# A two-layer transformer block on one core: where the low parts of the weights, one product, the first head copies and one mix stand in the engines' orders

## Time and profile before

| | |
|---|---|
| median of 3 runs | 876.03 us |
| profiled execution | 876.34 us |
| its span | 874.6 us |
| PE busy | 806.8 us (92%) |
| DVE busy | 667.3 us (76%) |
| ACT busy | 579.4 us (66%) |
| POOL busy | 422.2 us (48%) |
| mean granted PE clock | 0.985 |

### The profile page before, as it was taken

How to read it: one execution, slowest core, us unless ns; L and a number is a source line. 1 busy time by engine, 2 the same in 40 slices (tenths; PEclk the granted TensorE clock), 3 DMA queues, 4 the chain that set the end, 5 groups by cost and what they waited for, 6 DMA issues and landing times.

```text
span 874.6 us, 20901 instructions
## 1 busy us (share of the span) xinstructions
PE 806.8 (92%) x7097; PEld 677.9 (78%) x7097; DVE 667.3 (76%) x2136; ACT 579.4 (66%) x1232; POOL 422.2 (48%) x725
## 2 busy tenths in 40 slices
PE   4876999999999999899999999999998999999994
PEld 3554778888888899667777777777766988999984
DVE  5987889888896555778898888979886463487657
ACT  2777868687787533677878777777766233366646
POOL 0353223233253311576767667676765357355423
PEclk9899999999999999999999999999999899999998
DMA  7111220201001010111010211201013112345444
GB/s 218 35 40 43 80 86 12 87 14 37 26 1 49 25 38 25 43 34 31 22 55 23 63 42 37 66 22 43 23 59 120 37 64 95 92 129 134 128 161 170
DMA packets 55017, 54.86 MB, mean 63 GB/s; under 512 B 18209, under 2 KB 49185, under 8 KB 54914
## 3 DMA queue, kind: packets, MB, share of 16 engines
q1 hardware_dynamic: 51506, 44.18, 17.1%
q0 software_dynamic: 3408, 9.34, 3.1%
HBM read 32.85 MB, written 20.65 MB: 61 GB/s over the span
## 4 chain that ended last, share of the span: by engine, by line
PE 68%; DVE 15%; ACT 9%; issue 6%; POOL 1%; DMA 1%; DVEq 0%; ACTq 0%; SPq 0%; POOLq 0%
PE ps L448 13%; PE ps L449 12%; PE ps L450 12%; PE ps L992 10%; PE ps L1003 5%; PE ps L684 3%; PE ps L731 2%; DVE G L2182 2%; PE ps L771 2%; PE ps L976 2%; DVE wu_rows L2182 2%; ACT G L1596 1%; PE ps L1249 1%; PE ps L753 1%; PE ps L1213 1%
## 5 line engine op out<-in xcount | busy, mean ns | idle before, releaser
L2568 POOL TENSOR_SCALAR_AFFINE_SELECT G<-G 128x256 f32<-128x256 f32 x128 | 75.9, 617 | 150.1 <-ACT G L1422 149.9
L1596 ACT ACTIVATE G<-ps 128x512 f32<-128x512 f32 x184 | 102.7, 602 | 39.9 <-PE ps L992 38.3
L448 PE MATMUL ps<-WU 128*128 128x256 f32 x384 | 116.3, 303 | 11.4 <-DVE WU L1977 6.5
L2616 POOL TENSOR_SCALAR G<-G,small 128x256 f32<-128x256 f32 x214 | 99.8, 483 | 51.6 <-DVE small L2182 49.9
L2182 DVE CUSTOM_DVE_ANT_0 G<-ps,nb 128x256 f32<-128x256 f32 x296 | 108.3, 420 | 10.6 <-PE ps L731 9.4
L449 PE MATMUL ps<-WU 128*128 128x256 f32 x384 | 108.3, 282 | 0.0
L450 PE MATMUL ps<-WU 128*128 128x256 f32 x384 | 108.3, 282 | 0.0
L2616 POOL TENSOR_SCALAR wu_rows<-wu_rows,small 128x256 f32<-128x256 f32 x154 | 71.7, 482 | 38.7 <-DVE small L2182 37.7
L448 PEld LDWEIGHTS ps<-WU 128*128 128x128 f32 x384 | 72.8, 190 | 18.0 <-DVE WU L1977 7.3
L992 PE MATMUL ps<-ident,G 128*128 128x128 f32 x592 | 83.5, 278 | 3.0 <-ACT G L1596 2.9
L2182 DVE CUSTOM_DVE_ANT_0 wu_rows<-ps,nb 128x256 f32<-128x256 f32 x216 | 79.5, 420 | 7.4 <-PE ps L731 6.5
(11 more groups left out here) (267 smaller groups left out, 2356.2 us busy)
## 6 DMA issues: line engine op xcount, KB each, us to landing
xs<-G SPq DMA_DIRECT2D x8, 645.0 KB, 6.6
G<-xs SPq DMA_DIRECT2D x39, 128.0 KB
G<-x SPq DMA_DIRECT2D x17, 256.0 KB, 3.1
G<-in_x SPq DMA_DIRECT2D x16, 256.0 KB, 2.8
wu_rows<-yy SPq DMA_DIRECT2D x8, 512.0 KB, 7.0
x<-G SPq DMA_DIRECT2D x15, 256.0 KB, 2.2
wu_rows<-in_wu SPq DMA_DIRECT2D x8, 384.0 KB, 4.9
wraw<-in_wu SPq DMA_DIRECT2D x16, 128.0 KB, 2.2
```

The source lines that it names most:

```text
L448: pe.matmul(o, lh, rh, start=start, stop=False, skip_group_check=True)
L1596: act.activation(probT(n), halves(2 + n % 2), ACT.Exp).then_inc(probT_taken, 1)
L2568: m = pool.affine_select(out=u, in_=u, compare_op=ALU.is_ge, fill=0.0, base=0, pattern=[[0, 2], [1, P]], channel_multiplier=-1)
L2616: m = pool.tensor_scalar(p, p, -1.0, mneg[:, k:k + 1], ALU.mult, ALU.add)
```

## The change

Five edits, all in the order of existing calls; no operation is added or removed apart from waits.

1. **Low parts.** In batch 2 `raw_lo(p)` goes from behind the product (and, in slots 0 and 1, from behind `x1_lo`, `rope_half` and `rotated`) to ahead of `hidden_lo` and the product in DVE's slot.
2. **Slot 5.** `x_lo(0, i + 2)` goes from ahead of the product to right behind it, in batches 2 to 5.
3. **Head copies.** The first `q_heads` and `k_heads` of attention 2 stand at `k` 13 and 14 in place of 14 and 15.
4. **Mix by keys.** In slot 4 of attention 2 the first `mix_half` does only its lower keys at its old place; the upper keys follow behind `ct_turn`, right ahead of the second `mix_half`. In slot 6 of the last batch the first `mix_half` goes ahead of the second two `turn`s.
5. **End of attention 2.** Two of the last four `turn`s go ahead of the turning of the input block.

```diff
-                def mix_half(i, g, half):
+                def mix_half(i, g, half, keys=(0, 1)):
                     pe.wait_ge(probT_taken, H2 * i + 8 * g + 4 * half + 4)
-                    for kt in range(2):
+                    for kt in keys:
...
                             pe.wait_ge(o_copied[2], 4 * i + 1)
-                            mix_half(i, 1, 0)
+                            mix_half(i, 1, 0, (0,))
...
+                        if q == 6 and not left:
+                            pe.wait_ge(o_copied[2], 4 * i + 2)
+                            mix_half(i, 2, 0)
...
                                 ct_turn(2, i - 1)
+                            mix_half(i, 1, 0, (1,))
                             mix_half(i, 1, 1)
                         if q == 6:
                             if left:
                                 pe.wait_ge(v_staged[2], i + 2)
                                 turned(QS, DENSE_BANK, 0)
                                 pe.wait_ge(heads_k[2], 4 * (i + 1) + 1)
+                                mix(i, 2)
                             else:
-                                pe.wait_ge(o_copied[2], 4 * i + 2)
-                            mix(i, 2)
+                                mix_half(i, 2, 1)
...
                 pe.wait_ge(biased_ready, H2 * n)
+                for h in range(H2 - 4, H2 - 2):
+                    turn(H2 * (n - 1) + h)
                 pe.wait_ge(xt_loaded[3], 16)
...
-                for h in range(H2 - 4, H2):
+                for h in range(H2 - 2, H2):
                     turn(H2 * (n - 1) + h)
...
-                    if k == 14:
-                        q_heads(2, 0, 0)
-                    if k == 15:
-                        q_heads(2, 0, 1)
+                    if k in (13, 14):
+                        q_heads(2, 0, k - 13)
...
                         quartic(i, p - 1, not i)
+                    if i == LAG1:
+                        raw_lo(p)
                     if m >= 1:
                         hidden_lo(m - 1)
...
-                    if p == 5:
-                        if left > 1:
-                            x_lo(0, i + 2)
...
                     if m >= 0:
                         product(m)
+                    if p == 5 and left > 1:
+                        x_lo(0, i + 2)
...
-                    if i == LAG1:
-                        raw_lo(p)
...
-                    if k == 14:
-                        k_heads(0, 0)
-                    if k == 15:
-                        k_heads(0, 1)
+                    if k in (13, 14):
+                        k_heads(0, k - 13)
```

## The result

| | before | after |
|---|---|---|
| median | 876.64 us (4 runs, 875.99 to 878.23) | 868.97 us (4 runs, 867.93 to 869.82) |
| profiled execution | 876.34 us | 868.27 us |
| span | 874.6 us | 866.4 us |

The ratio after to before is 0.9909, 95% interval 0.9894 to 0.9923. The change makes the kernel 7.7 us faster by the medians and 8.1 by the profiled executions; 10.2 were forecast, 865.8 us, and the range (862.8 to 870.2) holds the result. (Before has one run more here than the three behind the 876.03.)

What follows compares the result with a forecast made beforehand. PE was taken to set the time, so gains come from its idle time. Terms 3.9 + 1.5 + 2.3 + 2.0 + 0 + 0.5 = 10.2 us took the median from 876.03 to 865.8 us, range 862.8 to 870.2.

Steps and rivals of the forecast that it cites:

- The signs named in the prediction: Trace marks of being right: gate_up(0) about 1 us behind scores, no half clock, listed waits gone, moved or new.
- The steps to scores(2, 2): Batch 2, slots 0 and 1: gate_up(0) starts 2.1 us earlier, at 82.85; with 1.7 from the clock, 3.8 earlier.
- The new wait in down(0): Batch 2: PE waits 1.4 us for hidden_lo, so gate_up(2) starts at 92.4, keeping 2.4 of the 3.8 us.
- slots 3 to 7: Batch 2: three more low-part waits, 3.2 us, end; 1.5 us taken as gain, bounds 0 and 3.2.
- The clock's term: Batch 2, 86.20 to 90.00 us: without the long idle, full speed in place of clock 0.55 saves 1.7 us.
- about 0.5 of each goes: Batches 3, 4 and 5: gate_up of slot 6 loses about 0.5 of each 0.53 us product wait; 1.5 us in all.
- the extra group of products: Attention 2, slot 4: a further change of product shape per slot costs 8 x 0.07, 0.6 us.
- Slot 6: Attention 2, last batch: half mix covers 0.65, other half waits about 0.74; gain zero, bounds -0.5 and 0.65.
- DVE becomes the bound: Rival, chance 0.2: in batch 2 the first wait only moves; low-part edit gives 1.0 to 1.5 us, time 868.4.
- The clock falls all the same: Rival, chance 0.06: falls in slots 0 and 1 leave 0.3 us, one in slot 3 costs 1.7; time 867.8.
- my reading of one stretch: Batch 2, 102 to 106 us: pauses, one wait of 1.31, clock 1.00; so a 1 us wait costs no clock.
- The slower rival: Rival, chance 0.03: late high parts hold DVE in batch 2, over 1.3 us in each of 8 slots; time 878.6.

Runs made afterwards that it cites:

- e5: Kernel before with only slot 6's half mix of the last batch and the last turns moved at the end of attention 2: 876.33 against 878.59 us, ratio 0.9989.
- b_again: Kernel before run once more, unchanged, for one more trace: 907.93 us (one run).
- c1: Changed kernel with slot 0's low part alone back behind x1_lo and rope_half: 870.95 us against 878.59 for the kernel before, ratio 0.9909.
- e2: Kernel before with only x_lo moved behind the product in slot 5: 904.84 against 904.88 us, ratio 1.0000.
- n1: Changed kernel with the second half of the heads' low parts in slot 6 behind the product: 896.59 us against 905.21 for the kernel before, ratio 0.9906.
- e1: Kernel before with only the low parts moved to the head of the slot in batch 2: 902.06 against 904.88 us, ratio 0.9969.
- n2: Changed kernel with hidden_lo ahead of the low part in batch 2: 897.48 us against 905.21 for the kernel before, ratio 0.9915.
- n3: Changed kernel with the moves of n1 and n2, plus slot 4's scale product behind the product: 865.03 us, ratio to the kernel before 0.9860.
- a_timed: Changed kernel, unaltered, timed on one chip beside n3 and the kernel before: 868.89 us against 878.59 for before, ratio 0.9902.
- a_again: Changed kernel run once more, unaltered, for one more trace: 897.89 us (one run).

## Why the prediction held, and where it did not

- **The whole.** The signs named in the prediction came: gate_up(0) 1.11 behind the scores with the clock at 1.00, a wait of 1.69 in down(0), none for the k copies, none of 0.30 in slot 4, 0.73 at the mix of slot 6. The sum was 2.0 too high for the spans (10.2 against 8.2): 0.8 of it in edit 1 and 1.4 in edit 2, with 0.2 back from the other three. That no fall of the clock came behind the new wait of 1.69 in the first trace was luck: it costs 1.4 where it comes.
- **The bound.** PE sets the time, and what is gained ahead of the expert stage stays gained: 8.20 us at its start, 8.2 in the span.
- **Edit 1, 3.9 forecast, 3.1 measured.** The steps to scores(2, 2) are right: gate_up(0) at 82.92 (82.85 forecast), the clock at 1.00, 3.63 us of lead (3.8). The new wait in down(0) was foreseen at 1.4 and is 1.69: DVE's rotated and centre took 1.45 and 1.31 where I had used 1.22 and 1.23, so that gate_up(2) is at 92.81 and not 92.4. In slots 3 to 7, for which I took 1.5 between 0 and 3.2, 1.15 came. The clock's term was right for the slot and too large for the batch: I counted 3.8 x 0.45 = 1.7, e5 shows 1.55 at scores(2, 2) and 1.1 at the end of the batch. It is also no fixed size: deeper falls cost up to 2.3 (b_again). c1 shows that slot 0 and its clock carry most of the gain, 3.3 of 4.0 us.
- **Edit 2, 1.5 forecast, 0.1 measured. This step failed**: "about 0.5 of each goes". I looked at the one wait, took the work that could hide x_lo's own lateness, and did not follow DVE to its next product. In before it stands 5.0 us further on (148.43 to 153.43), behind twelve instructions with no pause between them; it ended at 153.84, and gate_up of slot 7 started at 153.99. The 0.15 between them is what every released gate_up shows, so PE could come no earlier at all. e2 shows the wait moved and n1 that it goes when that product is freed.
- **Edit 3, 2.3 forecast, 2.1 measured** (2.6 alone, and 2.1 to 2.5 in three executions of the changed kernel): 2.4 at the first scores, 0.3 back at the second, where I had put 0.1.
- **Edit 4, 2.0 forecast, 2.5 measured in slot 4**, less 0.2 in slot 6. The wait of 0.30 comes back whole in seven slots, and 0.30 of the 0.74 in batch 0, where I had 0.5. The 0.06 for the extra group of products is there, but the mix starts as much earlier behind ct_turn, which I had not counted. Slot 6 traded 0.65 for 0.73 as foreseen.
- **Edit 5, 0.5 forecast, 0.6 measured.**
- **Rivals.** "DVE becomes the bound" had 0.2; it is what happened to edit 2 and to a part of edit 1, while it took too much from edit 1 (1.0 to 1.5 left; 3.1 were). "The clock falls all the same" did not come in the traces of the changed kernel but did in two that carry the same wait. The Trainium skill's rule on small pauses ("TensorE: Matmul & The Clock Gate", section "A second HAM failure mode: psum-queue depth-cycling") thus cannot be set aside by my reading of one stretch: PE was paused and kept the clock there, and lost it behind 1.70 us in e1. The section speaks of many small pauses, though, and this was one longer one; no run here separates the two. The slower rival showed once, at a third of its condition: DVE waits 0.41 us for a high part at 109.88, where over 1.3 in each of the 8 slots was asked.

## What to carry to other kernels

A wait that disappears is a gain only as far as the next meeting of the same two engines is late by less. Before pricing a reordering, follow the engine that was waited for to its next release and note by how much the waiting engine came after it, less the handover that rows with a wait show: if that engine runs without a pause, this margin (here 0.15 less 0.15, nothing) is the whole gain, whatever the wait was (0.53). Then look among the work in front of that release for what nobody needs yet; that, and not the order of two needed things, is what moved the end (n1, against n2; n3 has both and one move more).

## What the runs showed of the hardware

The clock's falls early in the kernel change from one execution to the next of the same program. They come behind long waits of PE, but not behind each: behind 3.1 us in 6 of 7 traces, behind 1.7 in 2 of 5. Earlier in the kernel 13 of the 14 traces have a wait of 1.62 us at about 48 (a_timed has one of 1.16 there) and all have one of 1.96 at about 70: behind the first the granted clock fell in 10 of the 13, behind the second in 9 of the 14. Behind the waits of 1.5, 1.6 and 1.23 us at about 56, 65 and 79 it fell in none. So the length of a wait does not decide by itself. What else does is open; e1 and n1, the two that fell behind the 1.7, are also the two of the five in which the clock had stayed at 1.00 from 68 to 76 us. In batch 2 a fall is worth 1.1 to 2.3 us, up to a quarter of what the whole change gained, so two traces are not enough to price an edit of that size.

On two of the chips the same kernels take about 28 us more (before 904.88 and 905.21 against 876.64), nearly all in one place: in the traces of e2, n1, a_again and b_again PE falls 26.4 to 26.6 us back at the work that stands at 725 to 733 us in before. e1 on one of them, waits of PE from 725 to 765 us, and the stretch from 730 to 760 (the first is total, times, longest):

```profile
PE ps L448 <- DVE g_split L2296: 8.4, 1, 8.4
```

```profile
730.00:760.00 30.00, 13.03 (x42) 9.77 (x42) 3.92 (x6) 3.44 (x7) 15.16 (x18) 0.54 0.25 84
```

PE is busy for 13.03 of 30 us there and for 29.60 in the same stretch of before on the first chip. The stretch is the one in which rows are scattered to the experts. What was gained ahead of it stays (a_again ends 11.3 us ahead of b_again on the same chip, and stood 9.4 ahead at the start of feed-forward 3, both counted from scores(2, 1)), so the lead passes through it; why it takes longer on these chips is open, and nothing was run on it.
